# VectorE's two-tensor operations moved between the two row maxima of a batch, in an attention kernel bound by TensorE

## The reference

```
xn   = group_norm(x, 32 groups)
mask = sigmoid(relu(mean(xn) @ w1 + b1) @ w2 + b2) > 0.5      # per image and channel
hyp  = logmap0(mhsa(expmap0(xn * mask), hdn weights))
euc  = mhsa(xn * (1 - mask), eu weights)
out  = x + hyp + euc
expmap0(u) = u * tanh(|u|) / |u|,  logmap0(y) = y * arctanh(min(|y|, 1 - 1e-5)) / |y|
```

## Time and profile before

| | |
|---|---|
| median of 3 runs | 4167.02 us |
| profiled execution | 4162.82 us, span 4161.1 us |
| TensorE busy, matmul | 3995.4 us (96%) |
| VectorE busy | 2696.5 us (65%) |
| ScalarE busy | 1950.4 us (47%) |
| GpSimd busy | 2698.4 us (65%) |
| mean granted TensorE clock | 0.998 |
| chain that ended last | TensorE 78%, VectorE 8%, issue 7%, GpSimd 5% |

### The profile page before, as it was taken

How to read it: one execution, slowest core, us unless ns; L and a number is a source line. 1 busy time by engine, 2 the same in 40 slices (tenths; PEclk the granted TensorE clock), 3 DMA queues, 4 the chain that set the end, 5 groups by cost and what they waited for, 6 DMA issues and landing times.

```text
span 4161.1 us, 69045 instructions
## 1 busy us (share of the span) xinstructions
PE 3995.4 (96%) x21822; PEld 2401.6 (58%) x21822; DVE 2696.5 (65%) x2643; ACT 1950.4 (47%) x3529; POOL 2698.4 (65%) x1311
## 2 busy tenths in 40 slices
PE   4999999999999999999999999999999999999999
PEld 3556565565655656565565655656556565565655
DVE  5665856668466684757746577465775658656586
ACT  4454534545345453544535445354553545435454
POOL 4584766847667475765757568575585746857377
PEclk9999999999999999999999999999999999999999
DMA  7212031120311203112031211311113111231212
GB/s 273 84 49 92 32 120 49 42 96 29 125 46 52 87 27 133 47 52 74 31 138 42 72 51 51 118 49 64 56 55 115 52 62 54 65 106 52 79 43 83
DMA packets 143726, 306.49 MB, mean 74 GB/s; under 512 B 17248, under 2 KB 30048, under 8 KB 133088
## 3 DMA queue, kind: packets, MB, share of 16 engines
q1 hardware_dynamic: 143328, 301.53, 21.1%
HBM read 251.15 MB, written 50.33 MB: 72 GB/s over the span
## 4 chain that ended last, share of the span: by engine, by line
PE 78%; DVE 8%; issue 7%; POOL 5%; ACT 1%; DMA 1%; SPq 0%; POOLq 0%; DVEq 0%; ACTq 0%
PE aux_ps L1235 28%; PE acc_ps L1347 18%; PE score_ps L1333 17%; PE aux_ps L1284 7%; PE score_ps L1235 4%; DVE mxp L1108 2%; POOL sums L637 2%; PE aux_ps L1357 2%; POOL xs L611 2%; DVE xin L1029 1%; ACT probs L810 1%; PE aux_ps L1294 1%; DVE den L1169 1%; DVE o_t L1174 0%; DVE sc L908 0%
## 5 line engine op out<-in xcount | busy, mean ns | idle before, releaser
L637 POOL TENSOR_TENSOR sums<-sums,probs 128x1024 f32<-128x1024 f32 x768 | 1861.3, 2424 | 810.6 <-ACT probs L810 770.3
L1108 DVE TENSOR_REDUCE mxp<-aux_ps 128x2 f32<-128x1024 f32 x1031 | 1262.4, 1224 | 1091.6 <-PE aux_ps L1284 1082.6
L810 ACT ACTIVATE probs<-score_ps 128x512 f32<-128x512 f32 x2048 | 1056.7, 601 | 656.5 <-PE score_ps L1333 649.2
L1347 PE MATMUL acc_ps<-probs,v_y 128*64 128x512 f32 x4096 | 991.8, 605 | 0.0
L1235 PE MATMUL aux_ps<-xs,w_qk 128*128 128x512 f32 x3072 | 834.3, 408 | 32.6 <-POOL xs L611 32.6
L1235 PEld LDWEIGHTS aux_ps<-xs,w_qk 128*128 128x128 f32 x3072 | 540.6, 188 | 421.8 <-issue 266.1
L637 POOL TENSOR_TENSOR sums<-probs 128x1024 f32<-128x1024 f32 x128 | 305.1, 2383 | 461.6 <-ACT probs L810 461.6
L1284 PE MATMUL aux_ps<-k_hi,q_hi 64*128 64x512 f32 x2062 | 471.5, 451 | 65.2 <-DVE mxp L1108 63.0
L1347 PEld LDWEIGHTS acc_ps<-probs,v_y 128*64 128x64 f32 x4096 | 248.3, 136 | 464.0 <-issue 419.7
L1169 DVE RECIPROCAL den<-den 128x256 f32<-128x256 f32 (+1 forms) x240 | 443.9, 1849 | 7.7 <-ACT den L821 7.7
L1333 PE MATMUL score_ps<-q_hi,k_hi 64*128 64x512 f32 x2048 | 406.8, 393 | 14.0 <-issue 14.0
(11 more groups left out here) (136 smaller groups left out, 3558.8 us busy)
## 6 DMA issues: line engine op xcount, KB each, us to landing
w_qk<-w_split SPq DMA_DIRECT2D x130, 512.0 KB, 4.1
xin<-in_x_dram SPq DMA_DIRECT2D x256, 256.0 KB, 2.9
w_o<-w_split SPq DMA_DIRECT2D x32, 1024.0 KB, 7.3
w_v<-w_split SPq DMA_DIRECT2D x32, 1024.0 KB, 5.9
v_y<-in_x_dram SPq DMA_DIRECT2D x72, 256.0 KB, 2.9
y<-v_y SPq DMA_DIRECT2D x64, 256.0 KB, 2.0
xin<-y SPq DMA_DIRECT2D x64, 256.0 KB, 2.9
out_dram<-v_y SPq DMA_DIRECT2D x64, 256.0 KB, 6.6
```

Of the source, the lines that this page charges most:

```text
L637: pool.tensor_tensor(sums[h][:, :], a, probs[:, g % SLOTS_P, :], ALU.add).then_inc(c_sum[h].sem, 1)
L810: act.activation(probs[:, n % SLOTS_P, token_half(u % 2)], score_ps[:, u % SCORE_BANKS, :], ACT.Exp, scale=SCALE).then_inc(c_exp.sem, 1)
L1108: dve.tensor_reduce(mxp[:, :, n, h], ps, AX.X, ALU.max).then_inc(c_free["D"].sem, 1)
L1347: last = nc.tensor.matmul(acc_ps[head(j), :], v_y[:, m, head(2 * p + j)], probs[:, n % SLOTS_P, token_half(j)], start=(m == 0), stop=(m == ...
```

## The change

It moves work in time; the arithmetic is the same.

- On VectorE, `o_lo`, `y_scale_step`, `operand_step` and `gate_step` now run in the middle of a batch, after the reduction of maximum 0 and ahead of `lows` and maximum 1. Statistics, square sums, `recip`, one reciprocal (`x_invert`) and `scale_x` of chunks 3 and 6 stay in the tail.
- Long groups of steps are dealt out over more batches: the y scale over b = 1 to 5, 26, 27 and 30, the x scale over b = 6 to 11. The reduction of the last y square moves behind maximum 0 of b = 0 (t = 1). y gets its own buffers `ss_y` and `sc_y`. `o_lo` comes one batch later.
- Two tiles of the gate come two batches earlier (b = 10 and 12). Squares of x start in b = 0 rather than 2. Masks start in b = 11 rather than 15; scaling, high part and low part of x have tables of their own, with one low part (GpSimd) a batch in b = 16 to 21, 23 and 24 (before: b = 18 one, 19 two, 20 one, 22 one, 23 two, 24 one).
- SyncE's order of loads follows: norm chunks 4 to 7 together at the start of t = 1, operand chunks 4 and 5 together.

```diff
-GATE_BATCH = {4: "mean", 6: "var", 12: "hidden", 14: "gate"}
+GATE_BATCH = {4: "mean", 6: "var", 10: "hidden", 12: "gate"}
-AGGREGATE, DEVIATIONS, RSTD_IN, RSTD, RELU, ABOVE, KEEP, SHIFT = 3, 5, 7, (9, 10, 11), 13, 17, 25, 29
-NORM_AT = {2: (0, 1), 3: (2,), 4: (3, 4), 5: (5,), 6: (6, 7)}
-CLAMP, POWER, ROOT, NORM, SERIES, EXP, SCALES, BLEND = 7, 8, (9, 10), 11, (8, 9, 12, 13, 14), 12, 13, 15
-MASK_AT = {15: (0,), 16: (1, 2), 17: (3,), 19: (4,), 20: (5, 6), 21: (7,)}
-Y_CLAMP, Y_NORM, Y_SCALE = 0, 1, 2
-DRAIN, DEN, MULT, SPLIT, LOW = 4, 5, 9, 10, 11
+AGGREGATE, DEVIATIONS, RSTD_IN, RSTD, RELU, ABOVE, KEEP, SHIFT = 3, 6, 7, (8, 9), 11, 14, 26, 27
+NORM_AT = {0: (0, 1), 1: (2,), 2: (3, 4), 3: (5,), 4: (6, 7)}
+CLAMP, POWER, ROOT, NORM, EXP, INVERT, SCALES, BLEND = 6, 6, (7, 8), 8, 8, 9, 10, 11
+SERIES = {6: (0, 1), 9: (2,), 10: (3, 4)}
+MASK_AT = {11: (0,), 13: (1, 2), 14: (3,), 17: (4,), 18: (5,), 20: (6,), 21: (7,)}
+SCALE_AT, SCALE_TAIL = {12: (0,), 14: (1, 2), 18: (4,), 19: (5,), 22: (7,)}, {15: (3,), 21: (6,)}
+HI_AT = {15: (0,), 16: (1,), 17: (2,), 18: (3,), 19: (4,), 20: (5,), 22: (6,), 23: (7,)}
+LO_AT = {16: (0,), 17: (1,), 18: (2,), 19: (3,), 20: (4,), 21: (5,), 23: (6,), 24: (7,)}
+Y_LAST, Y_CLAMP, Y_ROOT, Y_NORM, Y_SCALE = 0, 1, 2, 3, 4
+Y_SERIES = {5: (0,), 26: (1, 2, 3), 27: (4,)}
+Y_BLEND = 30
+DRAIN, DEN, MULT, SPLIT, LOW = 4, 5, 9, 10, 12
...
-                        load_chunks(i, 1, "norm", range(4, 6), next_image)
+                        load_chunks(i, 1, "norm", range(4, 8), next_image)
...
-                        load_chunks(i, 1, "norm", range(6, 8), next_image)
...
-                    load_chunks(i, t, "operand", range(4, 5), next_image)
+                    load_chunks(i, t, "operand", range(4, 6), next_image)
...
-                for j in MASK_AT.get(b - 3, ()):
+                for j in LO_AT.get(b, ()):
...
+                        if k == 0:
+                            pool.wait_ge(c_ysm.sem, c_ysm.at(i, 1))
...
-                        for j in MASK_AT.get(b - 2, ()):
+                        for j in HI_AT.get(b, ()):
...
+            def operand_tail(i, t, b):
+
                 for j in NORM_AT.get(b - 1, ()):
                     square_sum(i, t, j)
+                if b == INVERT:
+                    x_invert(i)
+                for j in SCALE_TAIL.get(b, ()):
+                    scale_x(i, t, j)
...
+                if b == Y_ROOT:
+                    dve.wait_ge(c_ya2d.sem, c_ya2d.at(i, 1))
+                    root(i, 0, sc[:, 0, :], ss_y[:, :], sc[:, 1, :])
+                    root(i, 1, sc[:, 0, :], ss_y[:, :], sc[:, 1, :])
...
                             max_slot(i, t, p, s)
                             if s == 15:
                                 combine(i, t, p)
-                            if j == 0 and b:
-                                lows(b - 1)
+                            if j == 0:
+                                if t and b == Y_LAST:
+                                    y_done(7, 0)
+                                if phase_at(b, LOW) is not None:
+                                    o_lo(phase_at(b, LOW))
+                                if t:
+                                    y_scale_step(i, b)
+                                    operand_step(i, t, b)
+                                else:
+                                    gate_step(i, b)
+                                if b:
+                                    lows(b - 1)
                         for ph, parts in recips(b):
                             recip(ph, parts)
-                        if phase_at(b, LOW) is not None:
-                            o_lo(phase_at(b, LOW))
                         if t:
-                            y_scale_step(i, b)
-                            operand_step(i, t, b)
+                            operand_tail(i, t, b)
                         else:
-                            gate_step(i, t, b)
+                            gate_tail(i, t, b)
+                    o_lo(2 * PAIRS - 3)
                     lows(BATCHES - 1)
```

More of the change, by code:

```diff
@@ L243, in build @@
         ss = sb("ss", [P, P])
+        ss_y = sb("ss_y", [P, P])
+        sc_y = sb("sc_y", [P, P])
         sc = sb("sc", [P, 4, P])
@@ L556, in _ @@
                     load_qk(t, 4, 0)
-                    load_chunks(i, t, "operand", range(4, 5), next_image)
+                    load_chunks(i, t, "operand", range(4, 6), next_image)
                     load_qk(t, 4, 1)
-                    load_chunks(i, t, "operand", range(5, 8), next_image)
+                    load_chunks(i, t, "operand", range(6, 8), next_image)
                     if t == 0:
@@ L859, in _ @@
                             act.wait_ge(c_yd2a.sem, c_yd2a.at(i, 1))
-                            power(i, sc[:, 0, :], ss[:, :], -0.5, c_ya2d)
+                            power(i, sc[:, 0, :], ss_y[:, :], -0.5, c_ya2d)
                         if t and b == Y_NORM:
@@ L970, in rstd @@
                     step(i, dve.tensor_scalar(small[:, 3, :], small[:, 3, :], -0.5, None, ALU.mult))
-                if part == 2:
                     dve.tensor_tensor(small[:, 0, :], small[:, 1, :], small[:, 3, :], ALU.mult).then_inc(c_pe_in.sem, 1)
@@ L1015, in x_norm, with x_invert, x_scale @@
                 dve.tensor_scalar(sc[:, 1, :], sc[:, 1, :], 20.0, None, ALU.min).then_inc(c_d2a.sem, 1)
-            def x_scale(i):
+            def x_invert(i):
                 dve.wait_ge(c_a2d.sem, c_a2d.at(i, 3))
                 step(i, dve.reciprocal(sc[:, 1, :], sc[:, 2, :]))
+            def x_scale(i):
                 step(i, dve.scalar_tensor_tensor(sc[:, 1, :], sc[:, 1, :], 0.5, sc[:, 0, :], ALU.subtract, ALU.mult))
@@ L1029, in scale_x, with gate_tail @@
                 dve.tensor_tensor(chunk, chunk, per_row(1, j * ROWS), ALU.mult).then_inc(c_xg.sem, 1)
-            def gate_step(i, t, b):
+            def gate_tail(i, t, b):
                 for j in STATS_AT.get(b, ()):
@@ L1036, in gate_step @@
                     aggregate(i, t)
+            def gate_step(i, b):
                 if b == DEVIATIONS:
@@ L1048, in gate_step, with operand_step @@
                     shifts(i)
-            def operand_step(i, t, b):
+            def operand_tail(i, t, b):
                 for j in NORM_AT.get(b - 1, ()):
                     square_sum(i, t, j)
+                if b == INVERT:
+                    x_invert(i)
+                for j in SCALE_TAIL.get(b, ()):
+                    scale_x(i, t, j)
+            def operand_step(i, t, b):
                 if b == CLAMP:
@@ L1059, in operand_step @@
                     x_norm(i)
+                for part in SERIES.get(b, ()):
+                    x_series(i, part)
                 if b == SCALES:
                     x_scale(i)
-                if b in SERIES:
-                    x_series(i, SERIES.index(b))
                 if b == BLEND:
                     x_blend(i)
-                for j in MASK_AT.get(b - 1, ()):
+                for j in SCALE_AT.get(b, ()):
                     scale_x(i, t, j)
@@ L1071, in y_scale_step @@
                     dve.wait_ge(c_sqf.sem, c_sqf.at(i, 8))
-                    dve.tensor_scalar(ss[:, :], ss[:, :], 2.0 ** -60, None, ALU.max).then_inc(c_yd2a.sem, 1)
+                    dve.tensor_scalar(ss_y[:, :], ss_y[:, :], 2.0 ** -60, None, ALU.max).then_inc(c_yd2a.sem, 1)
+                if b == Y_ROOT:
+                    dve.wait_ge(c_ya2d.sem, c_ya2d.at(i, 1))
+                    root(i, 0, sc[:, 0, :], ss_y[:, :], sc[:, 1, :])
+                    root(i, 1, sc[:, 0, :], ss_y[:, :], sc[:, 1, :])
                 if b == Y_NORM:
[L1074 to L1077, removed]
+                    step(i, dve.scalar_tensor_tensor(sc[:, 1, :], sc[:, 0, :], -0.5, ss_y[:, :], ALU.mult, ALU.mult))
                     dve.tensor_scalar(sc[:, 1, :], sc[:, 1, :], float(np.float32(1.0) - np.float32(EPS)), None,
@@ L1082, in y_scale_step @@
                     step(i, dve.tensor_tensor(sc[:, 3, :], sc[:, 2, :], sc[:, 3, :], ALU.subtract))
+                    dve.wait_ge(c_yread.sem, c_yread.at(i, 0))
                     step(i, dve.scalar_tensor_tensor(y_scale[:, :], sc[:, 3, :], -0.25, sc[:, 0, :], ALU.mult, ALU.mult))
[L1084 to L1088, removed]
+                for part in Y_SERIES.get(b, ()):
+                    if part == 0:
+                        step(i, dve.tensor_scalar(ss_y[:, :], ss_y[:, :], 1.0, None, ALU.min))
+                    series(i, part, sc_y[:, :], ss_y[:, :], ATANH_SERIES)
+                if b == Y_BLEND:
+                    blend(i, y_scale[:, :], sc_y[:, :], ss_y[:, :], ATANH_BELOW)
                     dve.sem_inc(c_ysm.sem, 1)
@@ L1127, in _ @@
             gate_read(None, -1, "var")
-            for part in range(3):
+            for part in range(2):
                 rstd(None, part)
@@ L1144, in _ @@
                 x_series(None, part)
+            x_invert(None)
             x_scale(None)
@@ L1181, in lows, with y_done @@
```

(12 more changed lines are left out.)

## The result

The changed kernel takes 4061.26 us (median of 4 runs, 4059.13 to 4061.72), the kernel before 4166.2 us in the same comparison: ratio 0.9748, 95% interval 0.9736 to 0.976. The forecast was 4072, in a range of 4054 to 4114.

What follows compares the result with a forecast made beforehand. TensorE was taken to bound the kernel, with only its waits for VectorE and GpSimd removable: 106 us off, 11 added, net 95; 4162.8 - 95 + 4.2 = 4072 us, range 4054 to 4114.

Steps and rivals of the forecast that it cites:

- What can go: TensorE's waits for VectorE's maxima and GpSimd's low parts of x: 106 us removable, 13.2 an image.
- the projections' waits: q/k projections in b = 20 and 24 wait for GpSimd's low part of x: 32.6 us, all gone.
- the 9 us that were to stay in the first batches of the halves: Second maximum follows its first with one tile of scores between: about 0.3 recorded plus 0.27, in 16 halves.
- The 0.27 a wait: Added to each of TensorE's 71 waits for VectorE, since a recorded 1.18 costs 1.45: 19 us in all.
- The cause: place against GpSimd's sums: VectorE's two-SBUF-input instructions and GpSimd's SBUF-reading ones exclude each other; between the maxima GpSimd is mostly idle, 0.9 us free.
- A late second reduction is hidden up to +4.58: In a plain batch the second maximum's reduction may start as late as 5.96 - 1.38 = +4.58 at no cost.
- What is added: Late reductions in second-half b = 19 (0.9), 7 (0.4) and 5 (0.1): 1.4 an image, 11 us, bounds 0 and 30.
- The second reduction was to start at up to +3.4: With `scale_x` or `o_lo` in the middle, the second maximum's reduction comes at up to +3.4 instead of +2.6, hidden.
- GpSimd always in a sum in the tail: In a batch's tail, from +3.75, GpSimd is always in a sum.
- The race: Rival: in b = 10, 14, 26, 30 GpSimd's sum beats the chain's last step; 23 us, 4095; chance 0.14.
- low part was late: Rival: chunks 3 and 7 still miss b = 20 and 24; some 36 us stay, 4108; chance 0.10.
- alternated with sums: Rival: a group of three in the middle alternates with two sums; 143 us, 4215, slower; chance 0.06.

Runs made afterwards that it cites:

- experiments 2 to 4: GpSimd's running sums cut to 128 of 1024 columns, in the wide-operations-in-tail kernel, the changed kernel and the kernel before: 4059.47, 4059.08 and 4058.75 us.
- experiments 1: Changed kernel with `o_lo` and all `scale_x` (two-tensor 128x512 operations) back in the tail, all else as changed: 4148.04 us.
- experiment 9: Changed kernel with the x scale's 128x128 steps back in the tail and ScalarE's two functions one batch later; wide operations stay in the middle: 4088.38 us.
- experiment 5: Changed kernel with high and low parts of x, masks, scalings and SyncE's load order as before; the rest stays in the middle: 4095.13 us.
- experiments 6, 7: Changed kernel with reciprocal and one or two dummy reductions in the middle of four first-half batches, delaying the second maximum's reduction: 4059.78 and 4091.46 us.
- experiment 3: Changed kernel with GpSimd's running sums over 128 of 1024 columns: 4059.08 us.
- experiment 8: Changed kernel with first y-series part moved to b = 4, first root step to b = 8, chunk 5 masked in b = 17 and scaled in 18: 4051.26 us.

## Why the prediction was right, step by step

- *What can go.* Predicted 106 us (13.2 an image) of waits and what their records hide. By batch lengths of the first seven images, 14.5 an image went, 116 us: 10.4 in the second half, most of it at b = 0 (0.70), 10 (1.59), 12 (1.20), 15 (0.77), 16 (0.82), 18 (1.43), 20 (1.67), 22 (1.34), 24 (0.62), and 4.1 in the first. Two terms were mis-sized. One is the projections' waits: 32.6 us were recorded and nothing was added for what the record hides, but b = 20 and 24 became shorter by 4.96 an image, 40 us. The other is the 9 us that were to stay in the first batches of the halves: b = 0 of the second half became 0.70 shorter, 5.6 us in all, since the square sum no longer stands ahead of its first maximum. The 0.27 a wait for the others was about right: b = 18 had 1.43 for a recorded 1.18.
- *The cause: place against GpSimd's sums.* Shown from both sides: with short sums the three orders are within 1 us of each other (experiments 2 to 4); put back the wide operations or the small ones alone and 87 or 27 us return (1 and 9). Short sums also empty GpSimd's list, so the times of 2 to 4 alone could mean that VectorE had waited for GpSimd's results. The durations say otherwise: it is the instructions of VectorE themselves that shrink (`scale_x` from 1648 to 722 ns), and a wait for a result lies ahead of an instruction. The 87, 34 and 27 us of experiments 1, 5 and 9 make 148 and not 105: they are prices in the changed kernel, and the first holds the pair in b = 19 with its loss of clock.
- *A late second reduction is hidden up to +4.58.* Shown: +4.60 (experiments 6, 7).
- *The tables of x.* Worth 34 us (experiment 5) beside the forecast's 32.6.
- *What is added.* Predicted b = 19: 0.9, b = 7: 0.4, b = 5: 0.1, 1.4 an image; measured 0.65, 0.36 and 0.17, 1.18 an image. The walk of GpSimd's list was 0.2 too pessimistic at b = 19 and gave the port all of it, where the mask is the larger part. So the lower bound of 0 was wrong as well: with short sums 0.4 of the 0.65 stays (experiment 3).
- *Missed without cost.* The second reduction was to start at up to +3.4. In b = 20 `o_lo` is issued just behind the start of a sum and takes 2.86 us; the reduction starts at +4.47 (+4.22 in the first half). The batch lasts 7.35 and hides it.
- *A reading that was too broad.* The prediction has GpSimd always in a sum in the tail. In the kernel before, the four scalings of b = 16, 18, 20 and 22, each behind a `recip`, took 0.63 us, and the four of b = 17 and 21 took 2.7 on average. The one at 2011.80 was issued 0.09 before a sum ended and ran ahead of the next, which then took 2.73. What decides is where the issue falls against GpSimd's list, and the tail only makes a bad moment likely.
- *The rivals.* The race was won in b = 10, 14, 26 and 30 (second reductions at +2.83 to +3.02); no low part was late; no group in the middle alternated with sums.
- *The sum.* In the trace the loop lost 13.3 us an image over the first seven, 106 us in eight, and the prologue was 3 us longer; the span is shorter by 103.7, where 95 was forecast.

## What to carry to other kernels

Where a VectorE operation shows several durations, ask which GpSimd instruction ran beside it, and lay it in the stretch where GpSimd is idle: here that was worth 2.5%, with no work removed. To learn how much such contention costs in all, make the other engine's operation short for one run; that gave 4059 us at once, nearly what the reordering reached (4061). It is an estimate and no limit: the short operation shifts the other engine's list (3.8 us in a new place here), and a better order without it went to 4051 (experiment 8). A delay costs nothing until a bank or an operand is wanted; work out that point from one plain batch and use the slack, but spend it in long batches.

## What the runs showed of the hardware that I had not expected

- Behind a single wait of TensorE of 3.85 us its granted clock was 0.50 (1.2 GHz), and the batch was 6.5 us longer; around a wait of 1.67 us in the same kernel (b = 15) it stayed at 1.00.
- The exclusion is not only for two-tensor operations: a `tensor_scalar` on one SBUF tensor of 128x128, 0.22 us in the changed kernel, took 2.21 beside a sum (experiment 9). A reduction of 128x1024 from PSUM (1.21 to 1.23 us in all 1031 of the changed kernel) and a reciprocal of 128x256 in SBUF (1.73 to 1.74 in all 224) keep their time beside GpSimd's sums.
- An instruction that waits inside its engine keeps its place: `x_lo` of GpSimd, issued 0.5 us ahead of VectorE's second scaling, ran between the two scalings, though these stand back to back in VectorE's list (experiment 8).
